# Two attention layers and two routed expert layers on one core: exp additions shifted to GpSimd, rows of maxima copied by two engines, ends of the attention layers pipelined by token half

## The reference

```python
x = x + attention0(ln(x))   # 12 heads of 32, all 1024 keys, relative positions, softmax, projection with bias
t = t + experts0(ln(t))     # router, best 2 of 8 experts, softmax over the two, gate, up, down
x = x + attention1(ln(x))   # 12 query heads, 4 key heads, window of 7x7 tokens, softmax, projection
t = t + experts1(ln(t))     # one shared expert for all tokens, and the best 2 of 8 experts
```

## Time and profile before

| | |
|---|---|
| Three runs | 1196.08, 1198.6, 1199.27 us; median 1198.6 |
| The profiled execution | 1194.93 us, its span in the profile 1193.4 us |
| Granted TensorE clock, mean | 0.951 of 2.4 GHz |
| Layer 0's attention blocks | about 91 to 312 us |
| End of layer 0's attention and routing | 312 to 376 us |
| Layer 0's experts | 376 to 556 us |
| Layer 1's attention blocks | 619 to 731 us |
| End of layer 1's attention, shared expert | 731 to 851 us |
| Layer 1's routed experts | 851 to 1165 us |

### The profile page before, as it was taken

How to read it: one execution, slowest core, us unless ns; L and a number is a source line. 1 busy time by engine, 2 the same in 40 slices (tenths; PEclk the granted TensorE clock), 3 DMA queues, 4 the chain that set the end, 5 groups by cost and what they waited for, 6 DMA issues and landing times.

```text
span 1193.4 us, 13523 instructions
## 1 busy us (share of the span) xinstructions
PE 1020.7 (86%) x4561; PEld 588.6 (49%) x4562; DVE 510.6 (43%) x898; ACT 319.4 (27%) x492; POOL 324.5 (27%) x281
## 2 busy tenths in 40 slices
PE   6999999999933999992778889799999999999990
PEld 3755454545511555551355556576444454445540
DVE  4566688786740444442634556711111111111113
ACT  3415554455320112210134544410011111111110
POOL 6425677776633011003110003350000001000005
PEclk9999999999975999997789999989999999999995
DMA  8699134000283345116160202333024414430005
GB/s 280 157 314 253 38 74 103 1 1 1 83 332 144 106 156 214 53 40 177 54 161 1 54 1 102 137 133 119 7 81 176 169 41 158 171 115 26 27 14 165
DMA packets 47114, 132.45 MB, mean 111 GB/s; under 512 B 6865, under 2 KB 25817, under 8 KB 46808
## 3 DMA queue, kind: packets, MB, share of 16 engines
q1 hardware_dynamic: 32424, 67.41, 19.6%
q0 software_dynamic: 14640, 64.36, 15.2%
HBM read 89.88 MB, written 30.87 MB: 101 GB/s over the span
## 4 chain that ended last, share of the span: by engine, by line
PE 69%; DVE 9%; issue 8%; DMA 6%; ACT 5%; POOL 2%; SPq 1%; POOLq 0%; DVEq 0%; ACTq 0%
PE PS L1674 20%; PE PS L1694 11%; PE PS L1472 5%; PE PS L1521 5%; PE PS L1398 4%; PE PS L1641 4%; DMA Wd<-in_Wd_r 4%; PE PS L1502 3%; DVE nmax_part L1156 3%; PE PS L1504 3%; PE PS L1605 3%; PE PS L1650 3%; ACT QB L946 2%; PE PS L1452 2%; DVE exp_acc L1188 2%
## 5 line engine op out<-in xcount | busy, mean ns | idle before, releaser
L1674 PE MATMUL PS<-Wgu,xbT 128*128 x690 | 277.6, 555 | 6.2 <-ACT xbT L1053 3.4
L1674 PEld LDWEIGHTS PS<-Wgu,xbT 128*128 128x128 f32 x690 | 131.4, 191 | 144.8 <-issue 133.0
L962 ACT ACTIVATE expS<-PS 128x1024 f32<-128x1024 f32 (+3 forms) x156 | 135.4, 878 | 135.2 <-PE PS L1504 131.5
L1694 PE MATMUL PS<-Wd,hidT 128*128 x414 | 145.6, 497 | 22.2 <-DVE hidT L1300 12.1
L798 POOL TENSOR_TENSOR exp_acc<-exp_acc,expS 128x512 f32<-128x512 f32 (+1 forms) x65 | 124.7, 1919 | 47.5 <-ACT expS L962 46.8
L1472 PE MATMUL PS<-KS,QA 128*128 128x512 f32 (+2 forms) x288 | 109.2, 426 | 18.8 <-DVE nmax L1156 6.8
L1502 PE MATMUL PS<-QA,KS 128*128 128x512 f32 (+3 forms) x312 | 116.9, 380 | 9.0 <-ACT QB L946 9.0
L1156 DVE TENSOR_REDUCE nmax_part<-PS 128x1 f32<-128x512 f32 x160 | 103.7, 685 | 46.0 <-PE PS L1472 45.2
L1071 ACT ACTIVATE hidT<-PS 128x384 f32<-128x384 f32 x46 | 22.5, 490 | 370.9 <-PE PS L1682 370.9
L1694 PEld LDWEIGHTS PS<-Wd,hidT 128*128 128x128 f32 x414 | 74.9, 189 | 75.6 <-issue 32.9
L1504 PE MATMUL PS<-QB,KS 128*128 128x512 f32 (+3 forms) x312 | 111.8, 364 | 0.0
(11 more groups left out here) (170 smaller groups left out, 1180.9 us busy)
## 6 DMA issues: line engine op xcount, KB each, us to landing
Wgu<-in_Wgu POOLq DMA_DIRECT2D x8, 1152.0 KB, 6.2
Wgu<-in_Wg_r POOLq DMA_DIRECT2D x8, 1152.0 KB, 6.3
Wgu<-in_Wu_r POOLq DMA_DIRECT2D x8, 1152.0 KB, 8.5
Wd<-in_Wd_r POOLq DMA_DIRECT2D x8, 1152.0 KB, 10.8
xb<-block_rows_in SPq DMA_DIRECT2D x46, 192.0 KB, 2.4
block_rows_out<-yb SPq DMA_DIRECT2D x46, 192.0 KB, 1.8
part_rows<-parts SPq DMA_DIRECT2D x2, 3072.0 KB, 17.9
Wd<-in_Wd POOLq DMA_DIRECT2D x8, 576.0 KB, 6.9
```

The source lines that it names most:

```text
L962: act.activation(exp_tile(layer, c, unit)[:, pair, :].rearrange("p (b n) -> p b n", b=2)[:, :, lo:hi], PS[:, 2 * pair:2 * pair + 2, lo:hi] ...
L1674: last = pe.matmul(PS[:, 3 * par + lo // BANK, 0:n], xbT[:, par, kc, :], Wgu[layer][:, bass.ds(s, 1), kc, lo:lo + n], start=kc == 0, stop= ...
L1694: last = pe.matmul(PS[:, 7, 0:C], hidT[layer][:, par, i, :], Wd[layer][:, bass.ds(s, 1), i, :], start=i == 0, stop=i == m.IC - 1)
```

## The change

Layer 0's additions: in units 1 to 4 of blocks 0 to 4 GpSimd adds all four heads (`POOL_ALL = 4`), VectorE none; in units 5 to 7 VectorE adds head 0 as before, after waiting for GpSimd's unit 4. In the last block the adds end with unit 5, and units 6 and 7 are summed directly (`DIRECT = 2`). The reciprocals of layer 0 read bank 7 themselves, and ScalarE's copy of the sums is gone there; in layer 1 it stays.

Rows of maxima: `maxima_rows` signals after each pair. ScalarE copies the first pair behind the last unit's first exp; VectorE copies the second in unit `ROWS_AT`, ahead of its reciprocal.

End of a layer: the projections of tiles 0 to 3 run inside the last block (in layer 0 behind units 5 and 6, in layer 1 behind units 3 and 4), their residuals too. VectorE computes the variances of half 0 before the last reciprocals and scales this half right after them. ScalarE's square root for half 0 stands ahead of its last copies. TensorE transposes both halves in a row, then does both router products, then the logits' transposes by halves. The banks are dealt out anew. In layer 0 GpSimd loads three experts before the scatter and the fourth behind it.

```diff
-        SUMS_AT = [2, 0]
+        POOL_ALL = 4
+        DIRECT = 2
-            return PER_HALF - 1 if hb < BLOCKS - 1 else PER_HALF - 2
+            return PER_HALF - 1 if hb < BLOCKS - 1 else PER_HALF - 1 - DIRECT
-        def dve_heads(hb):
-            return 1 if hb < BLOCKS - 1 else 2
+        def dve_heads(hb, v):
+
+            if hb == BLOCKS - 1:
+                return 2
+            return 0 if v <= POOL_ALL else 1
+
+        PROJ_V = [{5: (0, 1), 6: (2, 3)}, {3: (0, 1), 4: (2, 3)}]
+        RESIDUAL_V = [{6: (0, 1), 7: (2, 3)}, {4: (0, 1)}]
+        RECIP_V = [6, 4]
+        RECIP_V_LAST = [2, 1]
+        NORM_V_LAST = 3
...
-                early = 1 if layer else m.slots
+                early = 1 if layer else m.slots - 1
...
-                copy_sums(BLOCKS * (layer + 1) - 1)
+                root(2 * layer + 1, 0)
+                if layer:
+                    copy_sums(BLOCKS * (layer + 1) - 1)
                 copy_weighted(BLOCKS * (layer + 1) - 1)
...
-                    dve.wait_ge(sums_copied, hb + 1)
                     n, sums = BANK // cuts, norm_buffers(hb)[0]
+                    if layer == 0:
+                        dve.wait_ge(sums_psum, hb + 1)
+                        if hb >= 2:
+                            dve.wait_ge(normalised, normalised_before(hb - 1))
+                    else:
+                        dve.wait_ge(sums_copied, hb - BLOCKS + 1)
                     for i in range(cuts):
-                        dve.reciprocal(sums[:, i * n:(i + 1) * n], sums[:, i * n:(i + 1) * n]).then_inc(inverted, 1)
+                        src = PS[:, 7, i * n:(i + 1) * n] if layer == 0 else sums[:, i * n:(i + 1) * n]
+                        dve.reciprocal(sums[:, i * n:(i + 1) * n], src).then_inc(inverted, 1)
...
+                def copy_rows(hb):
+
+                    c = hb // HALF % KC
+                    dve.wait_ge(nmax_psum, 2 * hb + 2)
+                    dve.wait_ge(b_in[c % 2], placed(B_DMAS, layer, c))
+                    rows = 1 if layer == 0 else D
+                    for g in range(2, G):
+                        last = dve.tensor_copy(QB[layer][c % 2][D:D + rows, g, hb % HALF * BANK:(hb % HALF + 1) * BANK],
+                                               PS[D * g:D * g + rows, 4, :])
+                    last.then_inc(nmax_dve, 1)
...
+                variances(2 * layer + 1, 0, 1e-5)
                 reciprocals(end_block - 1, TAIL_CUTS)
+                scaled(2 * layer + 1, 0)
+                for t in range(NT // HALF, NT):
+                    residual(t)
+                normalise(2 * layer + 1, 1, 1e-5)
...
+                        direct = layer == 0 and last_block and v >= PER_HALF - DIRECT
+                        if direct:
+                            if v == PER_HALF - DIRECT:
+                                totals(BLOCKS - 1)
+                            direct_sums(u, v == PER_HALF - 1)
                         weighted(c, u)
...
+                        if last_block:
+                            for t in PROJ_V[layer].get(v, ()):
+                                project(t)
+                for t in range(NT // HALF, NT):
+                    project(t)
```

More of the change, by code:

```diff
@@ L1099, in normalise, with scaled @@
                 dve.tensor_scalar(var_eps[:, ts], mv[:, ts, 1], eps, None, ALU.add).then_inc(var_ready, 1)
+            def scaled(n, half):
+                tiles = range(NT // 2 * half, NT // 2 * (half + 1))
+                ts = slice(tiles[0], tiles[-1] + 1)
                 dve.wait_ge(std_ready, 2 * n + half + 1)
@@ L1104, in normalise @@
                                       ALU.subtract, ALU.mult).then_inc(xn_ready, 1)
+            def normalise(n, half, eps):
+                variances(n, half, eps)
+                scaled(n, half)
             def copy_transposes(n):
@@ L1415, in transposes, with transpose @@
                 layer = n // 2
-                for half in range(HALF):
-                    if n % 2:
-                        pe.wait_ge(proj_dve, NT * layer + 3 * (half + 1))
+                def transpose(half):
                     for kc in range(KC):
@@ L1494, in scores @@
                     if u % (U[layer] // 2) == 0:
-                        pe.wait_ge(nmax_act, 2 * (BLOCKS * layer + HALF * c + half) + pair + 1)
+                        pe.wait_ge(nmax_dve if pair else nmax_act, BLOCKS * layer + HALF * c + half + 1)
                     if use >= 2:
@@ L1528, in sums @@
                     first, last_one = u % (U[layer] // 2) == 0, (u + 1) % (U[layer] // 2) == 0
-                    if first:
-                        pe.wait_ge(sums_copied, 2 * (KC * layer + c) + half)
+                    if first and (c or half):
+                        pe.wait_ge(sums_copied, HALF * c + half)
                     for g in range(G):
```

219 lines of the change are left out of this document (131 added, 88 removed).

## The result

The changed kernel takes 1211.3 us (median of four runs, 1209.9 to 1212.9) beside 1197.3 us for the kernel before (four runs, 1194.5 to 1199.3). The ratio is 1.0119, with a 95% interval of 1.0091 to 1.0148: slower by some 14 us, where 1196 was forecast with 1187 to 1203 around it.

The account below looks back on a forecast made before the run. TensorE was busiest (86% of the span), so its waits were priced: -1.0 - 2.5 - 3.7 - 0.1 + 4.7 = -2.6 us on 1194.9, giving 1192.3; the median, 3.7 above, 1196.0. Own range 1192 to 1200; with rivals 1187 to 1203.

Parts of the forecast that it names:

- Additions, -1.0: Layer 0, blocks 0 to 4: moving adds to GpSimd gains 0.2 us a block, the rest lost meeting VectorE in unit 5.
- (a): Layer 0's additions keep their gain because the meeting in unit 5 fails to happen or costs nothing: 1189 us, chance 0.17.
- (c): GpSimd becomes layer 0's bound, waits lengthening its four-head units by 0.4 us each: 1204 us, chance 0.15.
- Rows of maxima, layer 0, -2.5: Layer 0's block boundaries: the second pair of scores no longer waits for ScalarE's second copy, 0.49 us gained five times.
- Rows of maxima, layer 1, -3.7: Layer 1's boundaries and first block: shorter waits for ScalarE's copy gain 4.0 us, less 0.3 for the later reciprocal.
- End of layer 0, -0.1: End of layer 0's attention: 1.3 us gained up to the scatter, 1.2 lost on the read; bounds 2.2 gained, 3 lost.
- the forecast's 1.9 and 0.2: End of layer 0: row_i 1.9 us earlier with router products at 2.4 GHz, 0.2 earlier with the slow stretch; 1.0 taken.
- 1.2 us back: End of layer 0: loss from the fourth expert's moved load meeting the first read of the sorted rows.
- End of layer 1, +4.7: ScalarE's root delays the sums' copy by 9.95 us; shared weights' loads hide 5.3, so the shared experts start 4.7 later.
- TensorE's own way gives 2.4 us later, so the weights decide: End of layer 1: TensorE's queue alone delays the shared experts 2.4 us; the late weight loads, 4.7 us, set their start.
- rival (d): New idle stretches at both layers' ends may leave TensorE at 1.2 GHz: 1 to 2 us each, inside the range; no chance given.
- Rival (b): The end of layer 1 costs nothing, as the root is not late or the weights have slack: 1191 us, chance 0.15.

Follow-up runs that it names:

- three fixes: Changed kernel plus second buffer in layer 1, fourth load behind the first read's transposes, and layer 1's last sums and reciprocals ahead of root and variances: 0.9925, 1187.7 us.

## Why the prediction was wrong

Predicted were -2.6 us; measured are +15.0 us in span. Point by point:

**Additions, -1.0.** Right in mechanism, too small in size. GpSimd is back to back, and VectorE's add in unit 5 takes 1.70 and ends behind GpSimd's. Forecast was 0.2 us a block of a possible 1.6; undoing the shift costs 0.6 in each of four blocks, some 2.3 us in all. Behind the start of the block's rows that add ends at 32.7 us (272.84 - 240.14), with the additions as before at 33.3; 33.2 was forecast. GpSimd's units took 4.78 us each instead of 4.86, so that its chain from unit 1 to unit 5 took 23.1 us with the waits, and not 23.4. Rivals (a), all of 8 us kept, and (c), GpSimd as the bound, both fell. With all seven units on GpSimd the blocks do get longer, but by VectorE's merge.

**Rows of maxima, layer 0, -2.5.** With the additions as before a block takes 38.1 us, 0.2 less than before the change: that is all that the rows of maxima and the reciprocals' new source bring, where 0.5 was forecast. The prediction put a second term at nothing without a reason: two passes over pairs cost TensorE 1.54 us where one pass took 1.08. In one pass a block is 0.5 us shorter. So the copies by two engines bring some 0.6 us a block, about as forecast, and the split pass takes most of it back.

**Rows of maxima, layer 1, -3.7.** This is the step that failed, and the largest miss: C is 8.1 us longer, so this term is off by 11.8. The sentence was that VectorE's "reciprocal is pushed back by as much; before, VectorE idles 1.80 us ahead of the next block's first reduction [...] which hides that", with 0.3 us off in layer 1 for the reductions. Three things are wrong in it. The push is 3.1 us, not 1.2, since the copy first waits 1.64 us for the second pass. The cover was read in layer 0 and carried to layer 1. And what waits for the reciprocal in layer 1 is not the reductions but, through product and copy, the one buffer. Some gain is there: with a second buffer C is 109.2 without the two projections, 3.3 below before. That this is near 3.7 is partly luck. Of the 3.3, 1.8 lies in the layer's first block (18.3 us instead of 20.1, at a granted clock of 1.00 instead of 0.92), where 0.6 was forecast. The five boundaries bring 1.5, where 3.1 was forecast, and here too the split pass, 0.4 to 0.5 us at each, was left out.

**End of layer 0, -0.1.** Measured +2.4 in B, within the bound of 3 lost. row_i came 2.4 earlier instead of 1.0, since the router's products, of which the first half had run at a granted clock of 0.61, ran at 1.00 here:

```profile
333.00:336.00 3.00, 3.00 (x8) 0.63 (x7) 0.56 (x1) 0.62 (x1) 1.45 (x3) 1.00 1.03 415
```

That is the luck of this trace. Of the nine traces of equal code up to there, eight have these products at 1.00 and row_i 68.1 to 68.6 us behind the last rows of maxima (70.5 before); the one with the fourth load behind the read has them at 0.79 and row_i at 70.2. Both cases are near the forecast's 1.9 and 0.2. But the scatter took only 1.1 of the 2.4, since it waits for the third load, whose chain I hadn't followed from the later reciprocals. And "1.2 us back" for the load beside the read was mis-sized: it costs 4.6 us. The highest landing of the earlier trace rows was 4.6, for a single read issued 6.8 us behind a load (417.35 and 410.55); here four reads stood together, the first 1.6 us behind a whole expert's weights. The Trainium skill's page DMA: Bandwidth & Descriptors (section Queues, rings and completion order) says that each DMA engine takes turns between its queues packet by packet; the first read landed at 378.2, behind the load's first two parts (375.6, 377.6) and ahead of its last (379.7), which agrees with it.

**End of layer 1, +4.7.** Right in sign, measured 6.4 in D, but through the other of the two ways. The hole ahead of projection 4 was forecast at 4.4 us and is 4.17. The step "TensorE's own way gives 2.4 us later, so the weights decide" failed: it took some 2 us off for the later work, and from the last projection to the shared experts nothing was saved (13.6 and 13.7 us). Most of that is TensorE's clock: the router's matmuls took 6.51 us at a granted clock of 0.81, and in the trace with the rows in one pass, where they took 5.32 at 1.00, the same way is 12.0 us. So TensorE's way decides, with the hole's 4.17, rival (d)'s 1.7 for projections that ran mostly at 1.2 GHz behind it, and 0.5 for eight projections that take 16.3 us in two parts and 15.75 in one. The cause of the hole was half seen: ScalarE's root was named, VectorE's own order was not, and moving the root alone brought the reciprocals forward by 0.8 us. Rival (b), no cost, fell.

**What the layer's ends brought.** With the fourth load behind the read B is 334.0 to 335.8 in three traces, 1.5 to 3.3 below before; D, with the 4.1 us, is 1.1 above with three fixes. So the new order gains in layer 0's end and nothing in layer 1's, even with both queues in order. What of B's gain is the pipelining by token half and what the later load is not separated.

## What to carry to other kernels

When an instruction is pushed back on an engine, follow its result to the buffer that it frees, and count the buffers of the stage in question: the slack read in one layer was worth nothing in the other, which had one buffer instead of two. When an engine's wait is blamed on the instruction ahead of it, look whether a second queue makes the same wait, because then the first repair alone shows little. And a load that is moved off one chain lands on the next transfer in time: issue it behind the read that the core waits for. Where a stage repeats a block, compare the period of the block and note the granted clock beside it: here that showed effects of 0.5 us a block which the stage's sum had mixed with one block's clock.

## What the runs showed that I had not expected

A VectorE instruction of 0.17 us can take 1.88 us beside GpSimd's adds (128x16 maxima, two inputs in SBUF). The Trainium skill's page SBUF — State Buffer (section SBUF: two separate sides) says that such an instruction, when GpSimd's started first, is blocked until that one has ended. The row agrees, with GpSimd's adds at 2.4 us each: a small VectorE instruction on the critical path can pay for most of a GpSimd instruction.

A 192 KB read issued 1.6 us behind an expert's load took 7.5 us, and the first five took 7.8 in the median instead of 2.6.

VectorE makes two copies of 32x512 out of PSUM in 1.39 us, ScalarE in 1.19: giving half of the copies to VectorE can pay only by the overlap.
